# Selective scan with routed ternary feed-forward: rows of B by DMA for the first two turns, and bf16 parts made by other engines

## What is computed

```
x_dbl = einsum('bld,kd->blk', x, W_xproj)          # 64 + 16 + 16 columns
Bmat, Cmat = x_dbl[..., 64:80], x_dbl[..., 80:96]
delta = softplus(einsum('blr,dr->bld', x_dbl[..., :64], W_dt) + b_dt)
deltaA = exp(delta[..., None] * A)
BX = delta[..., None] * Bmat[:, :, None, :] * x[..., None]
h = dA * h + bx                                    # scan over l
y = einsum('bdn,bn->bd', h, c) + D * x
```

## Time and profile before

| what | value |
|---|---|
| median of 3 runs | 346.23 us (344.85 to 347.11) |
| profiled execution, its own time | 345.58 us |
| span of that execution | 343.7 us |
| mean granted TensorE clock | 0.872 of full |
| DVE busy | 297.3 us (86%) |
| POOL busy | 271.7 us (79%) |
| PE busy | 251.1 us (73%) |
| ACT busy | 159.3 us (46%) |

### The profile page before, as it was taken

One profiled execution on the slowest core, in us unless ns is written; L12 is line 12 of the kernel. 1 busy time (PEld: TensorE's weight loads), 2 busy tenths in 40 slices (PEclk: granted clock), 3 DMA queues, 4 the chain that ended last, 5 costly groups with the idle time before them and its releaser, 6 DMA issues.

```text
span 343.7 us, 3843 instructions
## 1 busy us (share of the span) xinstructions
PE 251.1 (73%) x1183; PEld 144.1 (42%) x1184; DVE 297.3 (86%) x369; ACT 159.3 (46%) x216; POOL 271.7 (79%) x153
## 2 busy tenths in 40 slices
PE   0676498994968998979899798797970006999740
PEld 0422144441324654435565344453550003899640
DVE  1999999999999999999999997999989896656650
ACT  1375755447468565556445743333265501444210
POOL 0473988999888999999999959999937770377772
PEclk9995599997889999989999989898995555999885
DMA  7425799999998799988999773762001557898400
GB/s 243 132 75 185 251 297 300 359 376 317 315 373 273 265 331 311 301 307 296 330 314 317 259 237 106 259 219 97 2 1 52 196 212 260 286 291 270 155 2 0
DMA packets 36355, 78.80 MB, mean 229 GB/s; under 512 B 5027, under 2 KB 15789, under 8 KB 36336
## 3 DMA queue, kind: packets, MB, share of 16 engines
q1 hardware_dynamic: 23744, 63.15, 55.9%
q10 hardware_dynamic: 9776, 9.09, 8.2%
q0 software_dynamic: 2816, 6.32, 4.9%
HBM read 63.55 MB, written 17.09 MB: 235 GB/s over the span
## 4 chain that ended last, share of the span: by engine, by line
DVE 41%; PE 20%; issue 15%; DMA 9%; POOL 7%; ACT 6%; ACTq 0%; another core or an unknown queue 0%; SPq 0%; POOLq 0%; DVEq 0%
DVE xs_sb L788 16%; PE bank L1046 11%; DVE bank L783 9%; DMA xs_sb<-sorted_tokens 4%; PE bank L1011 2%; PE bank L1198 2%; POOL out_dram L457 2%; DMA x_sb<-in_L_attn_x_dram 2%; DMA out_dram<-cb,to_token 2%; POOL sorted_tokens L447 2%; ACT dA L562 2%; DVE st L817 2%; POOL xs_sb L400 1%; DVE xn L717 1%; POOL mask_sb L392 1%
## 5 line engine op out<-in xcount | busy, mean ns | idle before, releaser
L400 POOL TENSOR_TENSOR xs_sb<-xs_sb,cb 128x1024 f32<-128x1024 f32 x63 | 147.6, 2363 | 8.0 <-DVE xs_sb L788 5.3
L1046 PE MATMUL bank<-xs_sb,cst 128*128 128x512 f32 x256 | 130.8, 639 | 1.1 <-ACT xn L567 1.1
L788 DVE TENSOR_TENSOR_SCAN xs_sb<-dA,bank 128x1024 f32<-128x1024 f32 x44 | 100.6, 2286 | 1.5
L1046 PEld LDWEIGHTS bank<-xs_sb,cst 128*128 128x128 f32 x256 | 51.0, 205 | 47.5 <-issue 38.4
L783 DVE TENSOR_TENSOR bank<-bank,rows 128x1024 f32<-128x1024 f32 x44 | 53.3, 1210 | 0.1
L1011 PE MATMUL bank<-bc,pick 96*128 96x512 bf16 x88 | 30.3, 433 | 31.0 <-DVE xs_sb L788 31.0
L562 ACT ACTIVATE dA<-rows,a_neg 128x1024 f32<-128x1024 f32 x44 | 49.5, 1139 | 0.9 <-DVE rows L756 0.5
L457 POOL DMA_INDIRECT out_dram<-cb,to_token x32 | 31.8, 993 | 22.2 <-DVE cb L934 15.4
L392 POOL TENSOR_TENSOR xn<-xn,rows 128x1024 f32<-128x1024 f32 x16 | 37.6, 2352 | 5.4 <-DMA xn<-bc_rows 5.2
L788 DVE TENSOR_TENSOR_SCAN xs_sb<-bank,xn 128x1024 f32<-128x1024 f32 x16 | 36.3, 2271 | 0.3 <-ACT bank L562 0.2
L562 ACT ACTIVATE bank<-rows,a_neg 128x1024 f32<-128x1024 f32 x20 | 22.3, 1114 | 27.5 <-DVE xs_sb L788 27.5
(11 more groups left out here) (142 smaller groups left out, 335.7 us busy)
## 6 DMA issues: line engine op xcount, KB each, us to landing
cb<-bc_rows SPq DMA_DIRECT2D x63, 512.0 KB, 5.4
sorted_tokens<-wT SPq DMA_DIRECT2D x32, 257.0 KB, 10.7
xn<-bc_rows SPq DMA_DIRECT2D x16, 512.0 KB, 6.7
mask_sb<-_L_ffn_expert_masks_dram ACTq DMA_DIRECT2D x32, 256.0 KB, 5.8
xs_sb<-sorted_tokens SPq DMA_DIRECT2D x7, 1028.0 KB, 8.2
x_sb<-in_L_attn_x_dram SPq DMA_DIRECT2D x4, 512.0 KB, 7.7
mask_sb<-bc_rows SPq DMA_DIRECT2D x4, 512.0 KB, 5.7
xs_sb<-sorted_tokens SPq DMA_DIRECT2D x2, 514.0 KB, 4.3
```

The lines of the kernel that those rows point to most:

```text
L400: pool.tensor_tensor(prod[:, j, :], h[:, j, :], cb[:, j, :], ALU.mult).then_inc(s_prod, 1)
L788: dve.tensor_tensor_scan(h[:, j, :], decays, bx, 0.0, ALU.mult, ALU.add).then_inc(s_scan, 1)
L1046: mm = pe.matmul(yacc[:, c * HC:(c + 1) * HC], ident, prod[:, j, c * HC:(c + 1) * HC], start=first, stop=last, skip_group_check=True)
```

## The change

1. **Turns 0 and 1 take B by DMA** (`load_fed`). The two rows go into slots 2 and 3 of C's ring (`b_fed`), and DVE's multiplication reads them there. PE makes no `b_rows` for them. The C rows 2 and 3 are loaded once those multiplications are done (s_bx), and the B row of turn 5 stands behind them on SP's queue. The first multiplication also waits for the xnT copies that empty its PSUM banks.
2. **The parts for batch 0**: DVE makes the high part only; POOL subtracts (four instructions, before its first `bx`), ACT makes the middle part (two) and moves the middle and low parts (four, behind `decay(0)`). PE waits for them before the rows of turn 3.
3. **The parts for batch 1**: what DVE did at turns 8, 10, 11 and 13, ACT does at the same turns.
4. **pick and the bf16 identity** are made by POOL at its start, **a_neg** by ACT.
5. **POOL normalises 2 blocks** of 16 instead of 4 (`POOLED`), DVE two more.

```diff
-        POOLED = TB - 4
+        POOLED = TB - 2
+        FED = 2
...
+        def b_fed(k):
+            return cb[:, RING - FED + k, :]
...
+            def load_fed(k):
+                sp.wait_ge(s_dump, 16)
+                sp.dma_start(b_fed(k), bc_rows[0, k, :].partition_broadcast(P)).then_inc(s_bfirst[k], 16)
+
+            load_fed(0)
             load_c(0)
+            load_fed(1)
             load_c(1)
-            if pool_turns:
-                sp.wait_ge(s_xnps, 2 * DH * LH)
-                load_b(0)
-            load_c(2)
-            load_c(3)
-            if pool_turns:
-                load_b(1)
+            sp.wait_ge(s_xnps, 2 * DH * LH)
+            load_b(0)
+            for k in range(FED):
+                sp.wait_ge(s_bx, k + 1)
+                load_c(RING - FED + k)
+            load_b(1)
...
+            pool.wait_ge(s_xnpool, TB - POOLED)
+            for c in range(LH):
+                bc_subtract_high(0, c)
+            for c in range(LH):
+                bc_subtract_middle(0, c)
             for k in range(TURNS):
...
-            for q in range(DH * LH):
+            for q in range(DH):
                 xnT_out(1, q, bank[:, xn_bank[q], :])
+            for c in range(LH):
+                bc_middle(0, c)
...
             decay(0)
+            for q in range(DH, DH * LH):
+                xnT_out(1, q, bank[:, xn_bank[q], :])
+            for part in range(2):
+                for c in range(LH):
+                    bc_move(0, c, part)
...
+                if k in HIGH_AT:
+                    bc_high(1, HIGH_AT[k])
+                if k in MIDDLE_AT:
+                    bc_middle(1, MIDDLE_AT[k])
...
-            bc_parts()
+            for c in range(LH):
+                bc_high(c)
...
-                    dve.wait_ge(s_bready, of_dve[k] + 1)
-                    dve.tensor_tensor(bx, bx, u[:, dh, b * L:(b + 1) * L], ALU.mult).then_inc(s_bx, 1)
+                    rows_of_b = bx
+                    if k < FED:
+                        rows_of_b = b_fed(k)
+                        dve.wait_ge(s_bfirst[k], 16)
+                        dve.wait_ge(s_xnsb, DH * LH + DH)
+                    else:
+                        dve.wait_ge(s_bready, of_dve[k] - FED + 1)
+                    dve.tensor_tensor(bx, rows_of_b, u[:, dh, b * L:(b + 1) * L], ALU.mult).then_inc(s_bx, 1)
...
-                if k in HIGH_AT:
-                    bc_high(HIGH_AT[k])
-                if k in MIDDLE_AT:
-                    bc_middle(MIDDLE_AT[k])
...
-                if k + 1 < TURNS and k + 1 not in pool_turns:
+                if k + 1 == FED + 1:
+                    pe.wait_ge(s_bc3, 2 * LH)
+                if FED <= k + 1 < TURNS and k + 1 not in pool_turns:
                     b_rows(k + 1)
```

More of the change, by code:

```diff
@@ L199, in selective_scan_then_routed_ternary_ffn @@
         s_bload = [sem(f"b_loaded{j}") for j in range(2)]
+        s_bfirst = [sem(f"first_b_loaded{n}") for n in range(2)]
         s_gbx = sem("bx_ready_from_gpsimd")
@@ L369, in _ @@
             pool.memset(zero, 0.0).then_inc(s_zero, 1)
+            pool.wait_ge(s_cst, 16)
+            pool.tensor_tensor(pick[:, :], ident[0:96, 0:32], ident[0:96, 32:64], ALU.add).then_inc(s_pick, 1)
+            pool.wait_ge(s_pick, 1)
+            pool.tensor_tensor(pick[:, :], pick[:, :], ident[0:96, 64:96], ALU.add).then_inc(s_pick, 1)
+            pool.tensor_copy(ident_bf[:, :], ident).then_inc(s_idbf, 1)
             pool.wait_ge(s_late, 16 * LATE)
-            pool.wait_ge(s_cst, 16)
             pool.tensor_scalar(w_neg[:, :, :], w_nat[:, :, :], -0.25, None, ALU.is_lt).then_inc(s_sign, 1)
@@ L513, in delta_out, with bc_high, bc_middle, bc_move @@
                 act.activation(delta[:, dh, cols], delta_ps, ACT.Copy).then_inc(s_dsb, 1)
-            def bc_move(c, part):
+            def bc_high(b, c):
+                act.wait_ge(s_low, LH * b + c + 1)
+                act.activation(bc3[lanes, b * L + c * HC:b * L + (c + 1) * HC], xd[lanes, c * HC:(c + 1) * HC],
+                               ACT.Copy).then_inc(s_bchi, 1)
+            def bc_middle(b, c):
+                act.wait_ge(s_rest, LH * b + c + 1)
+                act.activation(bc_mid[lanes, c, :], bc_rest[lanes, c, :], ACT.Copy).then_inc(s_bcmid, 1)
+            def bc_move(b, c, part):
                 src = (bc_mid, bc_low)[part]
-                act.activation(bc3[32 * part:32 * part + 32, L + c * HC:L + (c + 1) * HC], src[lanes, c, :],
+                act.wait_ge((s_bcmid, s_bclow)[part], LH * b + c + 1)
+                act.activation(bc3[32 * part:32 * part + 32, b * L + c * HC:b * L + (c + 1) * HC], src[lanes, c, :],
                                ACT.Copy).then_inc(s_bc3, 1)
@@ L530, in _ @@
             act.activation(a_exp[:, :, :], alog[:, :, :], ACT.Exp).then_inc(s_amul, 1)
+            act.wait_ge(s_amul, 1)
+            act.activation(a_neg[:, :, :], a_exp[:, :, :], ACT.Copy, scale=-1.0).then_inc(s_a, 1)
             low_out(0, 0, bank[:, 4, :])
@@ L718, in norm_apply @@
                                       ALU.subtract, ALU.mult).then_inc(done, 1)
[L720 to L748 removed]
+            def bc_high(c):
+                dve.wait_ge(s_low, c + 1)
+                dve.tensor_copy(bc3[lanes, c * HC:(c + 1) * HC], xd[lanes, c * HC:(c + 1) * HC]).then_inc(s_bchi, 1)
             def delta_u(m):
@@ L762, in _ @@
             norm_apply(1, slice(0, LB), s_xn)
-            dve.wait_ge(s_cst, 16)
-            then_next(dve.tensor_tensor(pick[:, :], ident[0:96, 0:32], ident[0:96, 32:64], ALU.add))
-            dve.tensor_tensor(pick[:, :], pick[:, :], ident[0:96, 64:96], ALU.add).then_inc(s_pick, 1)
-            dve.tensor_copy(ident_bf[:, :], ident).then_inc(s_idbf, 1)
             norm_stats(slice(LB, TB))
             norm_apply(2, slice(LB, TB), s_xn, apply=POOLED)
-            dve.wait_ge(s_amul, 1)
-            dve.tensor_scalar(a_neg[:, :, :], a_exp[:, :, :], -1.0, None, ALU.mult).then_inc(s_a, 1)
-            bc_parts()
+            for c in range(LH):
+                bc_high(c)
             for m in range(2):
```

57 lines of the change are left out of this document (14 added, 43 removed).

## The result

| | before | after | ratio, 95% interval |
|---|---|---|---|
| first comparison, median us | 346.17 (344.43 to 349.62, 21 runs) | 344.08 (340.62 to 347.79, 21 runs) | 0.9928 (0.9907 to 0.995) |
| second comparison, another chip | 346.14 (344.42 to 347.91, 20 runs) | 341.78 (340.83 to 345.13, 6 runs) | 0.9895 (0.9853 to 0.9938) |

The changed kernel is 0.7 to 1.05% faster, 2.5 to 3.6 us. The forecast was 342.5. The profiled execution of the first comparison took 340.62 us (span 338.8), the fastest of its 21, so its trace shows more gain (5.0 us) than the medians do (2.1).

A forecast was written before the change was run, and what follows sets the result against it. DVE was taken to bound the turns, with the stream of rows expected next; 1.3 (start) + 0.3 (S) + 2.1 (POOL's idle) = 3.7 us off 346.23 gave 342.5, range 339.9 to 345.4, the forecast's own 341.5 to 343.7.

The forecast's parts named there:

- 1.3 us sooner: Scan of turn 1: waits for the second decay on ACT's queue, at 34.44 where it began at 35.77.
- S = +0.3: End of POOL's first product: the stream of C rows and zeros starts there, shifted 0.3 us sooner.
- 1.2 us apart: SP's queue at the start: pace of landing rows, putting the fourth at 30.3 and turn 2's B row at 31.5.
- 1.2 us at turn 1: Contention at the start: POOL's first product waits once for DVE's multiplication of turn 1, taking 1.2 from S = 1.6.
- The lead meets the stream at row 18: Row 18 of C lands at 99.5 with the queue full; POOL gains 1.3 + S = 1.6 us there, not 5.1.
- Rows over 2 us sooner by the clock: Sign that the forecast is wrong: rows of C landing over 2 us sooner by the clock.
- a first product that ends after 39: Sign that the forecast is wrong: POOL's first product ending after 39 us.
- The other 2.1 vanish: POOL from row 18's product on: its remaining 2.1 us of idle vanish, since DVE is far enough ahead (5.1 > 3.7).
- The stream does not bind: Rival, chance 0.25: the queue carries more, POOL follows DVE's whole 5.1 us lead: 341.1, up to 340.0 with S +1.6.
- The stream starts later: Rival, chance 0.2: C row 3 and B row 5 stand ahead of the stream, S = -1.5: gain 1.9, 344.3 us.
- The start is blocked: Rival, chance 0.1, turn 1: POOL's `bx` of turn 2 gets in before DVE's multiplication, S = -4.7: 347.5 us.
- without idle from 100 to 203: Sign for the forecast: POOL has no idle from 100 to 203 us, and DVE waits for POOL's `bx` or products.

The follow-up runs named there:

- subs_after_u: The changed kernel with POOL's batch-0 subtractions held back until DVE's two products of delta and x are done: 345.48 us, ratio to before 0.9991.
- after_again: The changed kernel unaltered, run once more on another chip (the second comparison): 341.78 us, ratio to the kernel before 0.9895.
- second trace: Trace of the changed kernel unaltered, from the second comparison; its profiled execution took 344.30 us.
- zeros_late: The changed kernel with the zeros written one block a turn in turns 12 to 43, not two in turns 0 to 15: 343.83 us, ratio to before 0.994.
- prod_first: The changed kernel with POOL's product(0) ahead of its `bx` for turn 2: 342.30 us, ratio to before 0.9911.
- b_zeros32: The kernel before with one block of zeros a turn in turns 0 to 31, not two in turns 0 to 15: ratio to before 0.9995.

## Why the prediction was right or wrong

**The total** was right: 342.5 against 344.08 and 341.78 by the two comparisons, inside 339.9 to 345.4. The first lies outside the forecast's own range of 341.5 to 343.7, the second inside. The sum of 3.7 us, 1.6 up to the product of turn 18 and 2.1 behind it, was near the 3.0 of the traces only because its terms erred both ways: by the clock that product starts 3.9 and 3.0 us sooner in the two traces, and behind it 0.5 is gained in the first and 0.9 lost in the second. That part is luck.

**DVE's start, "1.3 us sooner".** The mechanism held: the scan of turn 1 is bound by ACT's queue. It begins 12.96 or 12.97 us after the first softplus instruction in all ten kernels with the new start (subs_after_u apart); the forecast's 34.44 - 21.28 = 13.16 is 0.2 off. In kernels with the old start it begins 14.81 after DVE's second normalisation and does not follow ACT. But the forecast fixed the softplus at its time before, 21.28. It starts at 21.8 in the mean of those ten and at 21.4 in the three with the old start. The scan lies at 33.62 to 35.45, mean 34.7, and at 34.82 to 35.83, mean 35.5, in the three: 0.7 us sooner. The time of pick and identity does not reach ACT. DVE's timeline in after_again, its PE beside it:

```profile
20.67 0.17 DVE L751 TENSOR_TENSOR rr<-r 128x8 f32<-128x8 f32 x1 [1.60 <-ACT r L499]
```

```profile
16.75 4.64 PE L983 MATMUL bank<-xnT,wxT 128*96 128x512 f32 x8
```

DVE is ready sooner and waits 1.60 us for ACT's r, which stands behind a copy of PE's projection on ACT's queue. That projection takes 3.6 to 4.8 us from trace to trace; the first trace of the changed kernel had 3.60. Its softplus starts 1.8 us sooner than the second trace's, half of the 3.7 us between these two executions.

**"S = +0.3".** Wrong by nearly 2 us. Product(0) starts at 35.56 and 37.64 in the two traces (36.1 to 37.2 in the others with the new start and POOL's order, subs_after_u apart as from here on) against 34.7 to 35.4 with the old: about -1.5. The term that failed is the pace of rows, "1.2 us apart". Issued at 22.2, 22.6, 23.0 and 23.5, the first four landed 3.6, 5.9, 6.8 and 8.1 us later, that is at 25.8, 28.5, 29.8 and 31.6: 1.9 us apart, and the B row of turn 2 at 25.57 + 7.3 = 32.9 instead of 31.5. The landing rows of the first of the four and of the last:

```profile
DMA to landing us min/median/max: 3.6/3.6/3.6
...
DMA to landing us min/median/max: 8.1/8.1/8.1
```

That undoes the earlier issue: before, it went out at 29.3, 3.7 us later, and landed 3.7 us after, at 33.0. The first trace is the best case. Over the eight with the new start and POOL's order the B row lands 6.2 to 8.3 us after its issue, at 34.1 in the mean; in the three with the old start at 32.7. These 1.4 us are nearly all of the 1.5.

The contention was priced in the wrong place. The Trainium skill's rule ("SBUF — State Buffer", "Who interferes with whom") said it for two-input instructions; the prediction named the delta instructions by it but charged it once, 1.2 us at turn 1. The rows above bear the rule out, including that the second of a pair is held until the first is done. On DVE it came three times, at delta and at turn 0, 2.5 us, and it lengthened POOL's two middle subtractions to 3.4 us from 2.3; none of this reached the scan of turn 1 or product(0). Turn 1's multiplication, where the charge was placed, took 1.21. It came first, and POOL's `bx` beside it was held: 2.62 us instead of 2.34, so 0.3 (0.6 in zeros_late, nothing in the second trace).

**"The lead meets the stream at row 18".** Wrong in kind. Row 18 landed at 87.13 + 9.7 = 96.8 in the first trace, 2.7 us sooner than before, and POOL waited 0.24 us for it; in the second trace it waited for no row of C. "As the queue is full, an earlier issue does not land it earlier" is the step that fell: the stretch 76 to 101 carried 361 GB/s after and 334 before. Rows over 2 us sooner by the clock had been named as a sign of being wrong, and so had a first product that ends after 39, which the second trace shows (37.64 + 2.3 = 40.0). I had read the 11 us from issue to landing as the sign of a bound. zeros_late shows it to be none: its rows landed in 3.7 to 5.7 us between 58 and 76, and the turns were no faster. So up to row 18 the gain was 3.9 and 3.0 us and not 1.6: DVE's lead, won by the casts, took away POOL's waits at turns 15 and 17. The other side is prod_first, where this row did hold POOL for 1.30 us.

**"The other 2.1 vanish".** They did not, and the reason given, "DVE is far enough ahead", is the second step that fell. From the product of turn 18 to 203 us, but for the wait for the mask's buffer, POOL's idle was 2.0 us before and is 1.9 and 2.2 in the two traces. Its largest part is still the scan of turn 20, 0.83 and 1.09 us where it was 1.08, as in this row of the kernel before:

```profile
108.85 2.35 POOL L400 TENSOR_TENSOR xs_sb<-xs_sb,cb 128x1024 f32<-128x1024 f32 x1 [1.08 <-DVE xs_sb L788]
```

The idle that went lies nearly all ahead of turn 18: 5.8 us from the first product to there before, 2.6 and 1.3 after. In all POOL's idle fell from 12.3 to 8.5 us, 3.8, and its products by 0.6 with the casts gone. With -1.5 at product(0) that is 3.8 + 0.6 - 1.5 = 2.9 us. The two traces of the changed kernel end the turns at 240.7 in the mean, the two with the old start and DVE's casts (before, b_zeros32) at 243.7, 3.0 apart.

**The rivals.** "The stream does not bind" was the right mechanism, but it priced DVE's whole lead of 5.1 us, and 3.0 came. "The stream starts later" had S = -1.5 and 344.3 us, both close to what was measured in the first comparison, but by another cause: it put two rows ahead of the stream, and then let the stream bind. "The start is blocked" had the direction only: product(0) is later by 1.5 and not 4.7, through the landing of B's row; in the changed kernel DVE's multiplication came first, and not POOL's `bx`. The check "without idle from 100 to 203" failed too: 0.83 at 104.67, 0.51 at 137.84, 0.45 at 186.94 in the first trace.

## What to carry to other kernels

Where two engines alternate, ask for the lead of the one over the other and where it is used up, not for the clock time of the other's first instruction: product(0) 3 us sooner gave nothing, a scan of turn 1 3 us later cost 3, and four casts in turns 8 to 14 were paid as waits at turns 15 and 17. A full queue with long landings is not a bound until taking its load away makes the work faster. A total that comes out right does not vouch for its terms: compare each with the trace at the place where it was put. And look last for the largest wait that the change does not touch: here one constant moved by one turn ended the turns 1.5 to 2.0 us sooner from the softplus.
